# A recurrent block on one core: the product of gate and silu goes from VectorE to GpSimd, with other places for a few steps

## The reference

```python
xn = _layernorm(x)
x_norm = layernorm(xn, ln_in_g, ln_in_b)
x_norm = x_norm + depthwise_conv3_over_time(x_norm) + conv_b
gate = sigmoid(x_norm @ gate_w[:H].T + gate_b[:H])
Bm = x_norm * sigmoid(x_norm @ gate_w[H:].T + gate_b[H:]) @ B_w.T + B_b
Cm = x_norm @ C_w.T + C_b
A_bar = expm(dt_A * A)
def step(state, bc):            # 2048 steps, one after the other
    b_t, c_t = bc
    s = state @ A_bar + b_t
    s = _layernorm(s, ln_st_g, ln_st_b)
    return (s, c_t * s)
s = (ys @ D_w.T + D_b) * gate
g = silu(xn @ W.T + b + (xn @ V_r) @ C.T)
return x + s * g
```

## Time and profile before

| | |
|---|---|
| median of 3 runs | 2557.05 us (2556.99 to 2557.49) |
| profiled execution | 2557.63 us, its span 2555.8 us |
| TensorE busy | 2474.0 us (97%) |
| VectorE busy | 2201.8 us (86%) |
| GpSimd busy | 1275.3 us (50%) |
| ScalarE busy | 1006.8 us (39%) |
| granted TensorE clock, mean | 0.988 |

### The profile page before, as it was taken

The page is one execution under the profiler, slowest core; times in us unless marked ns, Lnnn a source line. Parts: engine busy times, 40 slices in busy tenths (PEclk is TensorE's granted clock), DMA queues, the critical chain, the costliest instruction groups (busy, mean ns, idle before and its releaser), DMA issues.

```text
span 2555.8 us, 42423 instructions
## 1 busy us (share of the span) xinstructions
PE 2474.0 (97%) x10001; PEld 1301.3 (51%) x10001; DVE 2201.8 (86%) x10937; ACT 1006.8 (39%) x1834; POOL 1275.3 (50%) x2485
## 2 busy tenths in 40 slices
PE   6899999999999999999999999999999999999986
PEld 3455555555555555555555555555555555555543
DVE  4688898888898888899888898888899888889876
ACT  3434344434334444334444344444344443334310
POOL 2355555455555455555455555455555455555442
PEclk8999999999999999999999999999999999999997
DMA  3111121121121122121122121122111122112112
GB/s 109 24 42 41 40 57 47 50 59 43 39 57 47 50 58 48 39 53 48 48 58 55 36 49 49 46 58 58 37 46 49 50 55 59 42 40 53 30 37 52
DMA packets 99798, 125.19 MB, mean 49 GB/s; under 512 B 32159, under 2 KB 48735, under 8 KB 99552
## 3 DMA queue, kind: packets, MB, share of 16 engines
q1 hardware_dynamic: 98912, 121.43, 19.4%
q10 hardware_dynamic: 640, 1.05, 0.2%
HBM read 71.96 MB, written 33.55 MB: 41 GB/s over the span
## 4 chain that ended last, share of the span: by engine, by line
PE 66%; DVE 15%; POOL 13%; issue 4%; ACT 0%; DMA 0%; DVEq 0%; POOLq 0%; ACTq 0%; SPq 0%
PE bank L986 17%; POOL dw L345 13%; PE bank L977 13%; PE bank L1019 8%; PE bank L969 7%; PE bank L1020 6%; DVE wq L752 6%; PE bank L996 4%; DVE dw L777 4%; DVE dw L763 4%; PE bank L1012 3%; PE bank L949 2%; PE bank L1003 2%; PE bank L959 2%; PE bank L926 1%
## 5 line engine op out<-in xcount | busy, mean ns | idle before, releaser
L345 POOL TENSOR_TENSOR dw<-q,minus_half 8x1 f32<-8x1 f32 x2048 | 1103.4, 539 | 1189.7 <-DVE wq L752 1158.7
L1019 PEld LDWEIGHTS bank<-Mscan,wT 128*65 128x65 f32 x2046 | 219.8, 136 | 670.4 <-issue 665.3
L977 PE MATMUL bank<-xnorm,gateT 128*128 128x512 f32 x1024 | 508.1, 595 | 0.0
L752 DVE SCALAR_TENSOR_TENSOR wq<-dw 8x65 f32<-8x65 f32 x2048 | 443.6, 217 | 70.5
L986 PE MATMUL bank<-xnorm,gateT 128*128 128x512 f32 x1024 | 500.9, 596 | 1.1 <-issue 1.1
L969 PE MATMUL bank<-xnT,WT 128*128 128x512 f32 x1024 | 495.2, 594 | 0.0
L1019 PE MATMUL bank<-Mscan,wT 128*65 128x128 f32 x2046 | 407.7, 281 | 36.9 <-DVE wT L780 24.6
L1020 PE MATMUL bank<-Mscan,wT 128*65 128x128 f32 x2046 | 392.9, 274 | 0.0
L777 DVE SCALAR_TENSOR_TENSOR dw<-dw 8x64 f32<-8x64 f32 x1024 | 279.8, 273 | 112.6 <-POOL dw L345 80.2
L767 DVE SCALAR_TENSOR_TENSOR dw<-bank,dw 8x128 f32<-8x128 f32 x1024 | 343.1, 335 | 24.8 <-PE bank L1020 22.4
L763 DVE SCALAR_TENSOR_TENSOR dw<-dw 8x64 f32<-8x64 f32 x1024 | 281.1, 275 | 90.8 <-POOL dw L345 82.5
(11 more groups left out here) (140 smaller groups left out, 2740.5 us busy)
## 6 DMA issues: line engine op xcount, KB each, us to landing
xc<-in_x SPq DMA_DIRECT2D x264, 128.0 KB, 2.8
out<-o SPq DMA_DIRECT2D x256, 128.0 KB, 2.4
xa<-in_x SPq DMA_DIRECT2D x248, 128.0 KB, 2.7
dw<-dtok SPq DMA_DIRECT2D x128, 96.0 KB
wtok<-dw SPq DMA_DIRECT2D x128, 33.0 KB
gateT<-in_gateT SPq DMA_DIRECT2D x1, 2048.0 KB
xa<-in_x ACTq DMA_DIRECT2D x8, 128.0 KB, 4.1
WT<-in_WT SPq DMA_DIRECT2D x1, 1024.0 KB, 6.0
```

Source lines behind the costliest of these rows:

```text
L345: nc.gpsimd.tensor_tensor(dw[0:B, t, CR:CR + 1], q[:], minus_half[0:B, 0:1], ALU.pow).then_inc(s["r_ready"], 1)
L752: V.scalar_tensor_tensor(out=wq[:], in0=w_eps, scalar=1.0 / S, in1=w_eps, op0=ALU.mult, op1=ALU.mult, accum_out=q[:]).then_inc(s["q_ready" ...
L977: ins = mm(mbank["gate", m][:], gateT[:, k, P * m:P * m + P], xnorm[p][:, k, :], start=(k == 0), stop=(k == KH - 1))
L1019: mm(scanP[0:WIDE, 0:2 * S], wT[:, 0:WIDE], Mscan[:, 0, :], start=True, stop=False)
```

## The change

Four things change. The product of gate and silu goes to GpSimd: `gate_silu` multiplies `TH` by `G` in four pieces of 128x128 for each of four tiles, each piece right behind the power of a step (t = 50 to 61, and for the fourth tile t = 1 to 4 of the next chunk; in the last chunk t = 36 to 51). ScalarE's `gate_tanh` adds one in a second pass, from the bank into `TH`, an SBUF tensor with room for two tiles. The bank is free after that pass. VectorE's `gated_silu` is gone.

GpSimd's layernorm operations are put in another order, so that the five that z needs come with the first 8, and `normalise_z` waits for these alone; chunk 0's own list stops there for the halo.

The wait for a quarter of d goes from the start of an even step to the end of the odd step ahead of it. `fill_d` has the places 46, 50, 54, 58, and `copy_dtok` of the second half stands behind `normalise_z`.

In the set-up, the convolution, the input gates and the other pieces have other places between the squarings; `b_proj` and `c_proj` of chunk 0 stand between the last squarings and not behind them.

```diff
-PE_D = (46, 48, 50, 52)
+PE_D = (46, 50, 54, 58)
-V_G = (49, 50, 53, 54, 57, 58, 61, 62)
+POOL_G = range(50, 62)
+POOL_G_NEXT = range(1, 5)
-V_G_LAST = (37, 38, 41, 42, 49, 50, 53, 54)
+POOL_G_LAST = range(36, 52)
-PE_WPRIME = (2, 3, 6, 7)
-DVE_WPRIME = (3, 4, 7, 8)
-PE_Z0 = (4, 4, 5, 5)
-DVE_CONV = (7, 8, 9, 10)
-PE_IG0 = (11, 11, 12, 12, 13, 13, 14, 14, 15, 15, 16, 16, 17, 17, 18, 18)
-PE_X0 = (13, 13, 15, 15)
-DVE_XG0 = (14, 16, 18)
-DVE_STATS2 = (16, 17, 18, 19)
+PE_Z0 = (2, 2, 3, 3)
+PE_WPRIME = (4, 5, 10, 11)
+DVE_WPRIME = (9, 10, 12, 13)
+DVE_CONV = (4, 5, 6, 7)
+PE_IG0 = (8, 8, 9, 9, 10, 10, 11, 11, 12, 12, 13, 13, 14, 14, 15, 15)
+PE_X0 = (10, 10, 12, 12)
+DVE_XG0 = (11, 13, 15, 17)
+DVE_STATS2 = (14, 15, 16, 17)
+PE_B0 = (14, 16, 17, 18)
+PE_C0 = (17, 18, 19, 19)
...
-                "gate": lambda: ("g_done", KH, i, k + 1),
+                "gate": lambda: ("gates_done", KH, i, k + 1),
...
+            def gate_silu(c, m, j, p):
+                if j == 0:
+                    wait_for(pool, "gates_done", KH, c, m + 1)
+                    wait_for(pool, "silu_done", KH, c, m + 1)
+                part = slice(P * j, P * (j + 1))
+                nc.gpsimd.tensor_tensor(G[p][:, m, part], TH[:, m % 2, part], G[p][:, m, part],
+                                        ALU.mult).then_inc(s["g_done"], 1)
...
                     if "F" in parts:
                         step(i, t)
+                        if "A" in parts and t in POOL_G:
+                            gate_silu(i, *divmod(POOL_G.index(t), NJ), i % 2)
+                        if "A" not in parts and t in POOL_G_LAST:
+                            gate_silu(i, *divmod(POOL_G_LAST.index(t), NJ), i % 2)
+                        if "C" in parts and t in POOL_G_NEXT:
+                            gate_silu(i - 1, KH - 1, POOL_G_NEXT.index(t), 1 - i % 2)
...
             def gate_tanh(c, m):
                 wait_for(act, "gate_mm", KH, c, m + 1)
                 a_(mbank["gate", m][:], mbank["gate", m][:], ACT.Tanh, scale=0.5,
-                   bias=v_("gate_b", m)).then_inc(s["gates_done"], 1)
+                   bias=v_("gate_b", m)).then_inc(s["tanh_done"], 1)
+                wait_for(act, "tanh_done", KH, c, m + 1)
+                wait_for(act, "g_done", KH * NJ, c, NJ * (m - 1) if m > 1 else 0)
+                a_(TH[:, m % 2, :], mbank["gate", m][:], ACT.Identity,
+                   bias=plus_one[:]).then_inc(s["gates_done"], 1)
...
-            def gated_silu(c, m, h, p):
-                if h == 0:
-                    wait_for(dve, "gates_done", KH, c, m + 1)
-                    wait_for(dve, "silu_done", KH, c, m + 1)
-                part = slice(TH * h, TH * (h + 1))
-                ins = V.scalar_tensor_tensor(out=G[p][:, m, part], in0=mbank["gate", m][:, part], scalar=1.0,
-                                             in1=G[p][:, m, part], op0=ALU.add, op1=ALU.mult)
-                if h:
-                    ins.then_inc(s["g_done"], 1)
...
-                if t % QT == 0:
-                    wait_for(dve, D_IN[t // QT], 16, i, 16)
+                if i == 0 and t == 0:
+                    wait_for(dve, D_IN[0], 16, i, 16)
...
+                if t % QT == QT - 1:
+                    of, q = divmod(i * NQ + t // QT + 1, NQ)
+                    if of < NC:
+                        wait_for(dve, D_IN[q], 16, of, 16)
```

More of the change, by code:

```diff
@@ L112, in build @@
         minus_half = sb("minus_half", [P, NJ])
+        plus_one = sb("plus_one", [P, 1])
         dbias = sb("dbias", [P, 1])
@@ L169, in build @@
             ig_mm igs_done xg_done b_mm dT_done dfill dtok_done c_mm cT_done
-            ffn_mm silu_done gate_mm gates_done g_done
+            ffn_mm silu_done gate_mm tanh_done gates_done g_done
             wr_done wrfill sn_done ys_done ssm_mm sg_done ofill o_done""".split() + OUT + D_IN + W_IN
@@ L212, in wait_for, with wait_ln @@
             eng.wait_ge(s[name], v)
+        def wait_ln(eng, n, k):
+            if n >= 0:
+                wait_for(eng, "ln_done", LN_OPS, n, k - (LN_OPS - LN_Z if n > 0 else 0))
         def hold(eng):
@@ L360, in ln_op @@
                     wait_for(pool, "xn_done", NJ, n - 1, 0)
-                wait_for(pool, "ln_done", LN_OPS, n, k)
-                if k == LN_OPS - 6:
+                wait_ln(pool, n, k)
+                if k == 3:
                     wait_for(pool, "z_done", NJ, n, 0)
@@ L369, in ln_op @@
                     lambda: g.tensor_scalar(nm, m0, scale[0], None, ALU.mult),
+                    lambda: g.tensor_scalar(both, var, scale[1] * (1.0 + EPS), EPS * EPS, ALU.mult, ALU.add),
                     lambda: g.tensor_scalar(a, var, scale[1], EPS, ALU.mult, ALU.add),
-                    lambda: g.tensor_scalar(both, var, scale[1] * (1.0 + EPS), EPS * EPS, ALU.mult, ALU.add),
+                    lambda: half_power(both, rr, 0),
+                    lambda: half_power(both, rr, 1),
+                    lambda: half_power(both, rr, 2),
+                    lambda: half_power(both, rr, 3),
+                    lambda: g.tensor_tensor(bz, nm, rr, ALU.mult),
                     lambda: half_power(a, r1, 0),
@@ L375, in ln_op @@
                     lambda: half_power(a, r1, 3),
[L376 to L379, removed]
                     lambda: g.tensor_tensor(bx, nm, r1, ALU.mult),
-                    lambda: g.tensor_tensor(bz, nm, rr, ALU.mult),
                 ][k]()
                 ins.then_inc(s["ln_done"], 1)
+            def gate_silu(c, m, j, p):
[5 more added lines that the diff above has]
+                                        ALU.mult).then_inc(s["g_done"], 1)
             for n in range(3):
-                for k in range(LN_OPS):
+                for k in range(LN_OPS if n else LN_Z):
                     ln_op(n, k)
@@ L419, in normalise_x @@
                 if tiles[0] == 0:
+                    wait_ln(act, c + 1, LN_OPS)
                     wait_for(act, "zfill", KH, c + 1, KH)
@@ L558, in _ @@
             copy_dtok(0, 1)
+            normalise_z(2)
             copy_c(0, 0)
-            normalise_z(2)
             def iteration(i, p, parts):
@@ L603, in iteration @@
                     gate_tanh(i, 1)
-                if A:
-                    copy_dtok(i + 1, 1)
                 if F:
@@ L609, in iteration @@
                     normalise_z(i + 3)
+                if A:
+                    copy_dtok(i + 1, 1)
                 if F:
@@ L635, in _ @@
             V.memset(ones[:], 1.0)
+            V.memset(plus_one[:], 1.0)
             V.memset(wT[:], 0.0)
@@ L855, in _ @@
                     bn_stats(2, DVE_STATS2.index(n), 1)
+                if n == DVE_STATS2[-1]:
+                    aggregate(2)
                 if n in DVE_XG0:
@@ L864, in _ @@
             assert done[0] == SETUP_M
[L866 to L869, removed]
             dve.wait_ge(s["pe_setup"], SQ_END + 1)
@@ L1060, in _ @@
                         fill_x(0, k, -1, False)
-            for piece in range(len(PE_IG0), KH * KH):
-                in_gate(0, *divmod(piece, KH), 0, -1, False)
-            pe.wait_ge(s["bt_steps"], 3)
-            for k in range(KH - 1):
-                b_proj(0, k, -1, False)
+                for k in range(KH):
+                    if PE_B0[k] == n:
+                        if k == 0:
+                            pe.wait_ge(s["bt_steps"], 3)
+                        b_proj(0, k, -1, False)
+                for k in range(KH):
+                    if PE_C0[k] == n:
+                        if k == 0:
+                            pe.wait_ge(s["wprime_done"], KH)
+                        c_proj(0, k, 0, -1, False)
             pe.wait_ge(s["dve_setup"], SETUP_M)
@@ L1073, in _ @@
             mm(scanP[0:B, 3 * S:4 * S], st_b_wide[:, 0:B], AC[:], start=True, stop=True).then_inc(s["pe_setup"], 1)
-            b_proj(0, KH - 1, -1, False)
             pe.wait_ge(s["dve_setup"], SETUP_M + 4)
@@ L1084, in _ @@
                 fill_d(0, q, -1, False)
-            pe.wait_ge(s["wprime_done"], KH)
-            for k in range(KH):
-                c_proj(0, k, 0, -1, False)
             pe.wait_ge(s["dve_setup"], SETUP_END)
@@ L1137 @@
 LN_OPS = 13
+LN_Z = 8
 SETUP_VEC = 7
```

19 lines of the change are left out of this document (8 added, 11 removed).

## The result

The changed kernel takes 2646.12 us (median of 4 runs, 2645.40 to 2647.49) against 2557.27 (2556.99 to 2562.52) for the one before: a ratio of 1.0346, 95% interval 1.0332 to 1.036. It is slower, within 6.1 us of the 2640 forecast. The profiled execution took 2645.4 us, 2.1 beyond its span.

A forecast was written before the change was run, and what follows sets the result against it. The ring of w, square sum and power was taken as the bound, 2442 of 2555.8 us. From 2557.6, repairs and set-up give -12.4 and pieces +94.7: 2640 us, 8 in 10 between 2543 and 2675.

The forecast's parts named there:

- the ring: One scan step: VectorE's w and square sum, then GpSimd's power -1/2; 1.18 to 1.19 us, taken as the bound.
- part 3: 512 pieces on GpSimd, whose reading holds w by 0.185 us each (0.134 to 0.237): 95 us; chance 0.49.
- Rival (a): w goes on while the piece reads, so pieces cost nothing: 2545 us; chance 0.27.
- Rival (b): w reads first or both take turns; a piece costs 0.034 up to 0.1 us: 2562 to 2596; chance 0.15.
- Rival (c): w waits until the whole piece has ended, 0.35 us each: 2724 us; chance 0.04.
- Rival (d): gates_done comes after the piece's place, so the next power, queued behind on GpSimd, is late: 2618 us; chance 0.05.
- Part 1: Places that hold the ring up: TensorE's lag from fill_d -7.1 us, third wait -3.4, VectorE's multiplication removed -0.4.
- the third wait: Every 16th step w also waits for d's landing, 0.055 us; moving it helps at steps 15 and 47: 3.4 us.
- Part 2: Set-up and first chunk: third step's wait gone, 3.5 us; first step 2.0 later; net -1.5, between -5 and +3.
- The stall at the third step: L767 waits 3.70 us for TensorE, which waits for late z; earlier z removes it, 3.5 us of the ring.

The follow-up runs named there:

- experiment 2: Changed kernel with each piece multiplying only 64 of its 128 columns: 2576.78 us.
- experiment 3: Changed kernel with each piece multiplying only 32 of its 128 columns: 2546.19 us.
- experiment 4: Changed kernel with each piece only on partitions 64 to 127, while w is on 0 to 7: 2697.6 us.
- experiment 5: Changed kernel with each piece replaced by a GpSimd memset of 256 columns of G that reads nothing: 2551.18 us.
- experiment 6: Changed kernel with each piece a tensor_scalar that reads TH only, one operand and not two: 2580.01 us.
- experiment 7: Changed kernel, 128x128 pieces kept, with w's second operand a constant in PSUM and not d in SBUF: 2743.34 us.
- experiment 8: Changed kernel with each piece waiting until the next step's w is written: 2652.74 us.
- experiment 1: Changed kernel without GpSimd's pieces and ScalarE's second pass; VectorE adds one and multiplies as before: 2544.64 us, 0.9946 of the kernel before.
- experiment 9: Against experiment 1, c_proj of chunk 0 put back behind fill_d in the set-up: 2545.28 us, 0.9942 of the kernel before.
- experiment 10: Against experiment 1, the set-up in its old order, z still after eight operations and ahead of cT: 2542.47 us, 0.9934 of the kernel before.

## Why the prediction was right

**The bound.** Right: every us of the difference is found in the ring's steps, in the set-up, or in the last chunk. A piece on an engine that was idle half the time, with room to spare, costs its price whole. The mechanism of part 3, reading on GpSimd that holds a `w` with two SBUF operands, is what experiments 2 to 8 show.

**Part 3, the price of a piece.** The forecast was 0.185 between 0.134 and 0.237, from one 128x4 operation that had held `w` by 0.034; measured 0.195, so 512 x 0.195 = 100 and not 95 us. The two steps of that estimate can be tested apart. The rate: I weighed 1.67 and 2.5 ns a column, taking two operands with or without the result; experiment 2 gives 2.1, and 3 doesn't contradict it. That I took the middle because I couldn't choose, and that 2.1 is the middle, is luck; neither of my two rates was right. The offset: 0.034 for four columns less 0.107 of an earlier start was sound, since by experiment 4 the price does move with the start. With 2.1 ns the prediction's own formula gives 0.034 - 0.107 + 124 x 0.0021 = 0.187, close to 0.195. The Trainium skill, page "GPSIMD Engine Reference", section "Elementwise — side-by-side cycle accounting", gives about 2.6 cycles an element for tensor_tensor on GpSimd; with the 1.2 GHz that the page states, that is an estimate of 2.17 ns an element. The pieces' growth of 2.1 ns a column agrees.

The piece: 0.40 to 0.50 us forecast, 0.445 measured.

**Rival (a), they don't meet,** is excluded by the trace after, and experiments 5 and 7 show what it would have needed: a GpSimd operation that reads nothing, or a `w` with one SBUF operand. **Rival (b), a short meeting,** is what pieces of 64 columns (0.060) or of one operand (0.036) are; at 128 it doesn't apply. **Rival (c), the whole instruction,** asked for 0.35, or 0.39 with the piece as long as it turned out. Measured 0.195, with the hold ending 0.19 us ahead of the piece's end, and in experiment 6 a longer instruction held less. The page "SBUF — State Buffer" of the Trainium skill, section "SBUF: two separate sides", names the right parties: a VectorE operation with two SBUF inputs against a GpSimd operation that reads SBUF. Experiments 5 and 7 agree with both conditions. Its "for the whole instruction" doesn't fit any row here. **Rival (d), a wait in GpSimd's queue:** none; the group of the piece shows 0.0 us of idling ahead of it.

**Part 1.** Forecast -7.1, -3.4, -0.4. Step 54, which held the wait for TensorE, lasted 1.42 us in the kernel before and lasts 1.18 in experiment 1. The waits of L767, now L787, for TensorE over the whole kernel, before and after (us in total, times, the longest), and two powers of the kernel after:

```profile
DVE dw L767 <- PE bank L1020: 22.4, 73, 3.7
...
DVE dw L787 <- PE bank L1038: 4.0, 9, 2.0
...
1058.71 0.54 POOL L354 TENSOR_TENSOR dw<-q,minus_half 8x1 f32<-8x1 f32 x1 [0.64 <-DVE wq L772]
...
1077.69 0.54 POOL L354 TENSOR_TENSOR dw<-q,minus_half 8x1 f32<-8x1 f32 x1 [0.70 <-DVE wq L772]
```

The last two are the powers of steps 16 and 32: the third wait's 0.055 us has left the one and stayed at the other, as forecast. A chunk without pieces gained 76.33 - 75.85 = 0.48 us in experiment 1, against 0.34 forecast (0.23 + 2 x 0.055). Step by step, 0.23 are at step 54 and 0.07 and 0.06 at steps 15 and 47, close to the forecast; the other 0.11 are 0.002 at each of the other steps. Chunks whose code is the same differ by as much between executions (75.85, 75.92 and 75.94 in experiments 1, 9 and 10), so I take no cause for them from these traces.

**Part 2 was mis-sized.** The stall at the third step, 3.5 us of the ring, went, as forecast. But the first step came 4.25 later and not 2.0, so the net is 4.25 - 3.5 = +0.75 and not -1.5. The rows of the kernel before, then of the kernel after:

```profile
76.87 0.27 PE L1069 MATMUL bank<-small,AC 64*64 64x1 f32 x2
...
81.96 6.36 SPq L269 DMA_DIRECT2D dw<-dtok  x4
...
86.23 0.27 DVE L763 SCALAR_TENSOR_TENSOR dw<-dw 8x64 f32<-8x64 f32 x1 [5.27 <-DMA dw<-dtok]
```

```profile
47.11 3.75 PE L1004 MATMUL bank<-xnorm,gateT 128*128 128x512 f32 x4 [1.05 <-issue]
...
80.26 0.27 PE L1092 MATMUL bank<-small,AC 64*64 64x1 f32 x2
...
85.37 7.21 SPq L278 DMA_DIRECT2D dw<-dtok  x4
...
90.48 0.27 DVE L783 SCALAR_TENSOR_TENSOR dw<-dw 8x64 f32<-8x64 f32 x1 [6.12 <-DMA dw<-dtok]
```

The gates start 52.57 - 47.11 = 5.5 earlier, as forecast. M's first product, at 76.87 in the kernel before, is at 80.26, 3.4 later: in this pair of traces what moved into the dense part was worth 8.9 us and not 7.7. The rest is d's landing, which I had costed at nothing: 5.11 us from its issue to the first `w`, and 81.96 to 86.23, 4.27, before. Neither difference can be laid to the order of the set-up from one pair, though: over the nine traces with the change's order the landing takes 4.29 to 5.12 us, and M's first product stands anywhere from 78.46 to 81.0. What holds over all traces is that the first power came at 89.85 to 92.41 us with the change's order and at 86.84 and 85.45 with the old one: 3.0 to 7.0 later, where I had said 2.0. Which term of the sum was too small stays open. The stall, too, is gone in only three of the nine: in the six traces in which the clock fell (experiments 2 to 7), the third step waits 1.3 to 1.4 us for TensorE and the fifth up to 0.8. The net of +0.75 is within the forecast's bounds of -5 to +3 and changed nothing of the sign.

**The sum.** Forecast -12.4 + 94.7 = +82.3. Measured in span: the repairs with the set-up -14.2 (2541.6 against 2555.8), the pieces +101.7, sum +87.5. The -14.2 is nearer to -12.4 than its terms are: the chunks gave some 4 us more than forecast, the set-up some 2 less.

## What to carry to other kernels

An engine's idle time is not free if what fills it shares a path with the operation that ends the critical wait: ask of a filler on GpSimd what it reads, how many columns, and whether a VectorE operation with two SBUF operands starts while it does. Short pieces (32 columns of two operands here; 64 already cost 0.06 us each) or operations that read nothing cost nothing here; longer reads belong elsewhere, as on VectorE beside the power, where this multiplication had cost nothing (a chunk of 75.85 us with it in experiment 1, 75.95 without it in experiment 5). When two edits come together, run each alone: here a gain of 14 us was hidden under a loss of 102. And before a shift of one or two us in a set-up is explained, read it in every trace that has the same set-up: here they differ by 2.6 us among themselves.

## What the runs showed of the hardware that was not expected

- A GpSimd operation queued behind a power doesn't always start at the same distance from the power's recorded end: a 128x128 tensor_tensor 0.02 us ahead of it, on partitions 64 to 127 0.08 behind it, a memset 0.04 ahead, and of three 128x4 tensor_scalars the first (L369) 0.01 ahead and the other two (L370, L371) 0.08 behind. The hold of `w` moved with it; the cause is open.
- On GpSimd a 128x128 tensor_scalar with one operand takes 526 ns, a tensor_tensor with two 445. A tensor_tensor is 242, 310, 445 ns for 32, 64, 128 columns: some 0.175 us and 2.1 ns a column.
- With the same set-up the granted clock of TensorE from 81 to 88 us was 1.00 in three traces and 0.50 to 0.69 in six, and `fill_d` took 1.57 us in the former and 2.93 in the latter. What decides between the two is open.
- With the second operand of `w` in PSUM, a VectorE operation behind it that reads PSUM too started 0.10 us later behind the square sum, and steps with further VectorE work took 1.27 to 1.42 us instead of 1.18; the cause is open.
